# Moving the second half of the next head's preparation from ahead of the strip stage to behind it, in an attention kernel with relative positions

## What is computed

```python
x = L0_attn_hidden_states
xn = layernorm(x)
s = L0_attn(xn)                      # 16 heads of 64, relative positions clipped to +-20
x = x + s * silu(L0_ffn(xn))         # int8-quantized 1024x1024
xn = layernorm(x)
s = L1_attn(xn)                      # chunked linear attention
x = x + s * silu(L1_ffn(xn))         # ternary weights, 1024->4096->1024

# L0_attn, for each head
idx   = clip(pos[None, :] - pos[:, None], -20, 20) + 20
attn1 = einsum('bhqd,bhkd->bhqk', q, k)
attn2 = einsum('bhqd,qkd->bhqk', q, rel_k[idx])
attn  = softmax((attn1 + attn2) / 8)
w1    = einsum('bhqk,bhkd->bhqd', attn, v)
w2    = einsum('bhqk,qkd->bhqd', attn, rel_v[idx])
out   = (w1 + w2) @ Wo.T + bo
```

## Time and profile before

| | us |
|---|---|
| median of 3 runs | 16955.04 (16923.59 to 16981.01) |
| the profiled execution, time | 16923.74 |
| its span, slowest core (core 1) | 16922.2 |
| spans of all cores | 16884.7 to 16922.2 |
| TensorE matmul busy | 6211.6 (37%) |
| VectorE busy | 5943.0 (35%) |
| ScalarE busy | 2240.2 (13%) |
| head loops of the two sequences, about | 1806 to 4811 and 9690 to 12724 |

### The profile page before, as it was taken

How to read it: one execution, slowest core, us unless ns; L and a number is a source line. 1 busy time by engine, 2 the same in 40 slices (tenths; PEclk the granted TensorE clock), 3 DMA queues, 4 the chain that set the end, 5 groups by cost and what they waited for, 6 DMA issues and landing times. The chain is left out here.

```text
span 16922.2 us, 87361 instructions; the slowest of 8 cores (16884.7 to 16922.2 us)
## 1 busy us (share of the span) xinstructions
PE 6211.6 (37%) x25317; PEld 2502.8 (15%) x25317; DVE 5943.0 (35%) x8678; ACT 2240.2 (13%) x2324; POOL 488.9 (3%) x846
## 2 busy tenths in 40 slices
PE   0013444444442233272042544444443323419014
PEld 0001111111110022031010211111111013204001
DVE  3632122222214465255712122222222455435651
ACT  0001211111111011021100112111210101103000
POOL 0130000000000000000000000000000000000000
PEclk9996555555566665586586755555555665559568
DMA  5533222222224300423114221212123320042311
GB/s 86 191 102 46 38 44 42 40 40 44 39 31 78 67 1 1 42 99 56 63 53 83 37 42 41 42 40 40 37 44 32 75 57 1 16 45 107 48 60 48
DMA packets 762244, 887.74 MB, mean 52 GB/s; under 512 B 446478, under 2 KB 657630, under 8 KB 715190
## 3 DMA queue, kind: packets, MB, share of 16 engines
q1 hardware_dynamic: 702022, 641.19, 15.4%
q0 software_dynamic: 59760, 240.97, 10.3%
HBM read 578.84 MB, written 294.16 MB: 52 GB/s over the span
## 5 line engine op out<-in xcount | busy, mean ns | idle before, releaser
L2247 PE MATMUL f_pD<-f_v,f_wd 128*128 128x512 bf16 x2048 | 557.2, 407 | 1915.9 <-DMA f_wd<-h_wdq 1911.8
L2076 PE MATMUL f_pG<-f_xq,f_wg 128*128 128x512 bf16 x2048 | 781.1, 381 | 738.5 <-DMA f_wu<-h_wuq 738.5
L2079 PE MATMUL f_pU<-f_xq,f_wu 128*128 128x512 bf16 x2048 | 780.9, 381 | 0.0
L961 PE MATMUL b_ptp<-sb_ident,b_h4t 128*128 128x128 bf16 x512 | 135.4, 265 | 1616.9 <-DVE b_h4t L939 1062.4
L939 DVE TENSOR_TENSOR b_h4t<-b_h4t,sb_adm 128x276 bf16<-128x276 bf16 x512 | 154.9, 303 | 1513.6 <-DMA b_h4t<-h_strip 1475.1
L895 ACT ACT_TABLE_LOAD x32 | 41.1, 1283 | 4270.6 <-PE b_pscA L886 4270.6
L850 DVE TENSOR_SCALAR b_kw<-b_qkt,relcols 64x128 bf16<-64x128 bf16 x512 | 127.6, 249 | 1313.7 <-PE b_pscB L886 1312.3
L895 ACT ACTIVATE b_aslab<-b_pscA 128x1024 bf16<-128x1024 f32 x512 | 524.3, 1024 | 485.4 <-PE b_pscA L886 225.3
L875 PE MATMUL b_pscA<-b_qkt,b_kw 64*128 64x512 bf16 (+2 forms) x832 | 384.1, 547 | 451.5 <-DVE b_kw L852 392.2
L895 ACT ACTIVATE b_aslab<-b_pscB 128x1024 bf16<-128x1024 f32 x512 | 522.7, 1021 | 69.9 <-PE b_pscB L886 67.5
L2247 PEld LDWEIGHTS f_pD<-f_v,f_wd 128*128 128x128 bf16 x2048 | 178.1, 101 | 2295.1 <-issue 2183.8
(11 more groups left out here) (392 smaller groups left out, 13697.6 us busy)
## 6 DMA issues: line engine op xcount, KB each, us to landing
h_gu<-f_gu POOLq DMA_DIRECT2D x64, 1024.0 KB, 4.2
f_gul<-h_gu SPq DMA_DIRECT2D x64, 1024.0 KB, 4.9
h_strip<-b_aslab SPq DMA_DIRECT2D x416, 100.8 KB, 10.5
b_h4t<-h_strip SPq DMA_DIRECT2D x512, 69.0 KB, 1.8
p_wc<-wgT SPq DMA_DIRECT2D x16, 2048.0 KB, 10.6
p_wc<-wuT SPq DMA_DIRECT2D x16, 2048.0 KB, 10.2
p_wc<-wdT SPq DMA_DIRECT2D x64, 512.0 KB, 3.6
a_xc<-x SPq DMA_DIRECT2D x32, 1024.0 KB, 4.8
```

Source lines behind the costliest of these rows:

```text
L961: tensor.transpose(ptp2[:, 0:128], sl[:, 0:128], ident[:])
L2076: tensor.matmul(pG[n % 2][:, q * 512:(q + 1) * 512], wgb[sg4 % 2][:, wcol:wcol + 128], xsl, start=(ich == 0), stop=(ich == NCH - 1))
L2079: ins = tensor.matmul(pU[n % 2][:, q * 512:(q + 1) * 512], wub[sg4 % 2][:, wcol:wcol + 128], xsl, start=(ich == 0), stop=(ich == NCH - 1))
L2247: ins = tensor.matmul(pD_[:, qt * 512:(qt + 1) * 512], wdb[n % 2][:], v2slab[:, oc * T + qt * 512:oc * T + (qt + 1) * 512], start=(oc == 0 ...
```

## The change

The call of `mid_hook()` moves from between the scores and the strip stage to between the strip stage and the attention-value stage. No instruction is added or taken away; on each engine the instructions of `l0_r1b(h+1)` now stand behind those of head h's strip stage.

```diff
@@ -896,8 +896,6 @@
                                             psc[n % 2][:], AT.Exp, scale=0.125), 'scs', 1)
             blk_all.scalar(s_scalar)
 
-        if mid_hook is not None:
-            mid_hook()
         if True:
             ptp2 = pst['ptp2']
             if True:
@@ -974,6 +972,8 @@
                         c.inc(gp.dma_start(out=dst, in_=srcs), 'h6g', 16)
                 blk_all.gpsimd(s_gp)
 
+        if mid_hook is not None:
+            mid_hook()
         if True:
             pOa = pscA[0:65, 0:512]
             pOm = pscA[0:65, 512:1024]
```

## The result

The changed kernel takes 16230.6 us (median of 9 runs, 16144.9 to 16274.6), the kernel before 16980.6 (10 runs, 16923.6 to 17042.2): 0.9552 of it, 95% interval 0.9531 to 0.9573, 750 us less. The forecast was 16134 us, range 16000 to 16310; the measured time lies 97 us above it, and 26 of these come from the kernel before, whose median is 16980.6 with ten runs in place of 16955.0 with three. Against the forecast ratio, 1 - 821/16955 = 0.9516, the measured one is 0.0036 higher: the direction and the main term held, the gain was some 70 us smaller. The profiled execution has spans of 16101.6 to 16171.3 us (before 16884.7 to 16922.2).

A forecast was written before the change was run, and what follows sets the result against it. The path was a 34 us idle stretch between scores and strip stage, strip stores queued behind `l0_r1b` on SP. 922.8 - 12 - 90 = 821 us off 16955.0 gave 16134 us, range 16000 to 16310.

The forecast's parts named there:

- The gap: Between scores and strip stage: TensorE's 35.08 us wait falls to 5.06, transposes leave; gain 30.76 us a head, 922.8 in all.
- the changed kernel in small: Last head of each sequence, without hook: strip stores issue during the scores and TensorE waits only 5.06 us.
- SP catching up: During the scores: strip stores start late, about three strips waiting, but SP catches up, 0.79 us issue against 3.2 a strip.
- Traffic beside the scores: Strip stores beside exponentials and score matmuls: a cost of 0.4 us a head, 12 us in all, perhaps nothing.
- `l0_r1b` in its new place: Between strip stage and attention-value stage: `dgt2` loads delayed, a cost of 3 us a head, 90 us in all.
- the `dgt2` loads come behind them on the same queue: On SP's queue before line 1024: `dgt2` loads start behind the still running `cstr` loads, +2.1 to +4.1 us.
- the bounds: On the `dgt2` delay: 0 to +8.7 us a head (262 us), including GpSimd's stores stretched by a microsecond or two.
- The bandwidth fit: For the `cstr` bulk: 3.4 us to landing, delay near +0.5 us; judged far too short against the trace's 6.9 us.
- Slack and clock: Next head's `cstr` has 56 us of cover before its scores; shortening the gap shouldn't change TensorE's 0.71 clock grant.
- its rival: Attention-value stage: TensorE's clock falls to 0.50, up to 11.5 us a head or 344 us, 16478; chance 0.03.
- The slower rival: SP stands in `l0_r1b`'s landing wait while TensorE waits for `dgt2`, over 30.8 us a head; 17555 at 60 us; chance 0.02.
- no effect: Between scores and strip stage: a wait the last head lacks holds the strips back, gap stays, 16955; chance 0.02.

The follow-up runs named there:

- pv_early: Changed kernel with transposes and copy of `l0_r1b` back ahead of the strip stage, SP part left as changed; 16192.9 us, 0.9523 of the kernel before.
- no_overlap: Changed kernel, but SP issues no strip store before the head's last exponential; 16691.0 us, 0.9828 of the kernel before.
- sp_late: Changed kernel with the `ptil` store and `cstr` loads moved behind the first six `dgt2` loads; 16144.1 us, 0.9500 of the kernel before.
- cstr_late: Changed kernel with only the `cstr` loads moved behind the first six `dgt2` loads; 16172.1 us, 0.9521 of the kernel before.
- again: The changed kernel run once more with no edit; 16208.8 us, 0.9538 of the kernel before.

## Why the prediction was right, and where not

1. *The gap* (922.8 us forecast). Gap waits fell from 1065.8 to 168.4 us in the mean over the cores; with the 22.2 us of transposes moved away that is 919.6. The term was right to 0.4%, and its account, SP's order, is shown by pv_early; the last head was the changed kernel in small (5.06 us there, 5.3 a head now). Of what the term says about SP catching up, the end is right and a detail wrong: line 907 took 9.3 us to issue right behind line 793's store, whose landing took 18.2 us on this core (12.6 before; 13.3 and 12.1 as medians over all cores), and the strip stores began some 21 us after the table load. They still caught up.
2. *Traffic beside the scores* (12 us forecast as a cost). Nothing: head 7 takes 50.57 us from table load to last exponential with the stores, head 8 took 50.50 without, and ScalarE's wait in the page's row is 225.3 us in both kernels, and in no_overlap.
3. *`l0_r1b` in its new place* (+3 us a head, 90 us forecast). The size was nearly right: the `dgt2` wait grew by 104.6 us, and it begins 0.74 us later a head, so 127 us or 4.2 a head; in the second execution 99.6 or 3.3. The mechanism was wrong. The step that failed is "the `dgt2` loads come behind them on the same queue": the `dgt2` loads weren't issued until GpSimd's third store had landed, at 3081.46 in head 7, when `cstr` had landed (issued by 3075.42, 5.7 us at most to its landing in this trace), and they took 2.98 us there, as before; in the mean they took 0.26 us more, of the 4.25 that were added. What is late is the step ahead of them, GpSimd's `h_h6` stores, which have the other 3.98; the prediction named this in one sentence and left it in the bounds. sp_late takes all of it away, cstr_late a third. That the size came out near 3 us is luck: it was worked out from a landing of 6.9 us for `cstr`, which in its new place took 4.4, and from a queue that the loads didn't meet.
 The rule of the Trainium skill that was cited (DMA: Bandwidth & Descriptors, section on queues, rings and completion order: engines take turns between queues) agrees with GpSimd's stores slowing down under SP's traffic; its other half, ring order within a queue, had nothing to decide here. The bandwidth fit of that page (section on the anatomy of one DMA) would give `cstr` 3.4 us, an estimate, since the page measured it on DMAs that GpSimd issues and SP issues `cstr`; the measured 4.4 is nearer to that than the 6.9 of the earlier trace rows, which had strip stores behind it.
4. *Slack and clock.* The next head's `cstr` lands at about 3080, the next scores start near 3147: no wait appeared. TensorE's busy time in line 1017 is 441.1 us (440.0 in the page before). Head 7 alone would mislead: over the 48 us that answer to the earlier trace rows TensorE was granted 0.61 where it had 0.71. Over the same stretch of all heads with a hook on all cores the mean is 0.66 (0.65 before) and the matmul busy time 28.5 us (28.8 before), so the clock in that stage did not fall, and its rival is out. The slower rival and "no effect" never had a sign.
5. *The sum.* 919.6 - 126.8 = 793 us by the waits, 787 measured in the head loops (mean of the cores), 821 forecast. The rest, down to 750 in the medians, lies outside: in the profiled pair the other stages are 15 us longer in the mean, and the slowest core stands further from the mean (38 us against 18). The long gate product of cores 0 to 3 in that execution is part of it; since "again" has a normal one and a median only 22 us lower, I don't claim it as the cause.

## What to carry to other kernels

In a program where one engine issues most DMAs, read the time from its point of view: list its waits in program order and ask which transfers behind each wait were ready. A wait for a chain that isn't urgent belongs behind the issues that are, and a place in the program where no such chain exists (here the last head) prices the change. When transfers are moved, look for the stores and loads that they will now run beside, on any queue, before looking at the queue itself: here moving them once more, past the urgent loads, was worth about another 0.4%, and letting the first loads go ahead of the last store 0.7%.

## What the runs showed that was not expected

Two SP transfers of short rows slowed GpSimd's stores. The `ptil` store (rows of 82 bytes) took the two stores of 512 KB from 3.73 and 3.56 us to 4.53 and 4.58 in the mean (sp_late against cstr_late), and over 6 us in one head of five; the `cstr` bulk load (rows of 336 bytes) took the small third one with its wait from 2.38 to 3.87 us (cstr_late against again). An issue on SP can take long right behind a large transfer of short rows: line 907 took 7.2 to 13.6 us to issue in every head with a hook, behind line 793's 508 KB in rows of 254 bytes, and 0.7 us in the two heads where line 793 isn't there; in the kernel before, where it came some 50 us after line 793, 0.8 to 2.1 us. And the pace of the strip stage varies between executions and variants for no reason found: the waits inside it are 554.9 us in the kernel before (mean of the cores), 560.6 and 589.6 in two executions of the changed one.
